# Attention scores of two streams as two 64-row tiles of TensorE, with split masks and per-slot clearing

## The reference

```python
q1, q2 = _apply_rope(q[..., :hd]), _apply_rope(q[..., hd:])      # 16 heads, hd = 8, two streams
k1, k2 = _apply_rope(k[..., :hd]), _apply_rope(k[..., hd:])
a1 = softmax(where(causal, neg, einsum('bhqd,bhkd->bhqk', q1, k1) * scale))
a2 = softmax(where(causal, neg, einsum('bhqd,bhkd->bhqk', q2, k2) * scale))
out = einsum('bhqk,bhkd->bhqd', a1 - lam * a2, v)                # then RMS norm per head, Wo, bo
```

## Time and profile before

| | us |
|---|---|
| median of 3 runs | 2002.75 (1998.85 to 2003.01) |
| the profiled execution | 2003.73 |
| its span, first to last instruction | 2001.9 |
| first feed-forward | to about 436 |
| attention | about 436 to 1566 |
| second feed-forward | about 1566 to the end |

### The profile page before, as it was taken

How to read it: one execution, slowest core, us unless ns; L and a number is a source line. 1 busy time by engine, 2 the same in 40 slices (tenths; PEclk the granted TensorE clock), 3 DMA queues, 4 the chain that set the end, 5 groups by cost and what they waited for, 6 DMA issues and landing times. The chain is left out here.

```text
span 2001.9 us, 38651 instructions
## 1 busy us (share of the span) xinstructions
PE 1846.7 (92%) x14144; PEld 1377.4 (69%) x14144; DVE 1391.4 (70%) x3443; ACT 1278.7 (64%) x1613; POOL 1035.0 (52%) x693
## 2 busy tenths in 40 slices
PE   4999999964899999999999999999998399999999
PEld 3788788843567676776776676766765277777777
DVE  5777777755767777777777777777762377777775
ACT  4777777741266666666666666666656277777776
POOL 5888888833233333424233333334221388888885
PEclk9999999986899999999999999999999599999999
DMA  3233333222222213122222222132210233333331
GB/s 106 106 106 107 106 106 106 97 83 57 56 67 57 78 49 83 52 75 62 65 68 61 73 54 79 47 82 55 69 42 14 85 125 106 107 106 106 107 101 59
DMA packets 141249, 158.76 MB, mean 79 GB/s; under 512 B 12706, under 2 KB 123442, under 8 KB 140338
## 3 DMA queue, kind: packets, MB, share of 16 engines
q1 hardware_dynamic: 141060, 156.28, 25.8%
HBM read 91.20 MB, written 14.70 MB: 53 GB/s over the span
## 5 line engine op out<-in xcount | busy, mean ns | idle before, releaser
L971 ACT ACTIVATE att_prob<-att_ring 128x1024 f32<-128x1024 f32 x384 | 389.3, 1023 | 265.6 <-PE att_ring L1186 260.9
L1096 DVE TENSOR_REDUCE att_nmax<-att_ring 128x4 f32<-128x1024 f32 (+1 forms) x384 | 457.5, 1220 | 125.9 <-PE att_ring L1186 122.7
L292 POOL TENSOR_TENSOR ffn_h_low<-ffn_h,ffn_h_high 128x1024 fp32r<-128x1024 f32 x192 | 458.5, 2401 | 95.1 <-ACT ffn_h_high L341 94.9
L479 DVE TENSOR_TENSOR ffn_h<-ffn_up,ffn_comb_wide 128x1024 f32<-128x1024 f32 x256 | 311.3, 1216 | 125.8 <-ACT ffn_up L334 121.3
L334 ACT ACTIVATE ffn_up<-ffn_up 128x1024 f32<-128x1024 f32 x256 | 258.1, 1008 | 202.9 <-PE ffn_up L567 201.6
L1186 PE MATMUL att_ring<-att_kd,att_qs 102*128 102x512 bf16 (+1 forms) x1024 | 304.4, 332 | 17.9 <-DVE att_nmax L1096 6.6
L1186 PE MATMUL att_ring<-att_qs,att_kd 102*128 102x256 bf16 (+1 forms) x2048 | 284.8, 248 | 14.6 <-DVE att_nmax L1096 8.0
L341 ACT ACTIVATE ffn_h_high<-ffn_h 128x1024 fp32r<-128x1024 f32 x256 | 269.4, 1052 | 0.7 <-DVE ffn_h L479 0.7
L1186 PE MATMUL att_ring<-att_mask,att_ident 128*128 128x256 bf16 x1024 | 262.3, 277 | 0.0
L897 POOL TENSOR_TENSOR att_qk<-att_turned 128x512 f32<-128x512 f32 x64 | 81.1, 1268 | 338.1 <-DVE att_turned L1075 338.1
L1186 PE MATMUL att_ring<-att_mask_t,att_ident 128*128 128x256 bf16 (+1 forms) x768 | 239.3, 312 | 0.0
(11 more groups left out here) (140 smaller groups left out, 2896.3 us busy)
## 6 DMA issues: line engine op xcount, KB each, us to landing
ffn_comb_wide<-ffn_comb_d SPq DMA_DIRECT2D x128, 512.0 KB, 5.6
att_qs<-att_parts SPq DMA_DIRECT2D x192, 128.0 KB
att_kd<-att_parts SPq DMA_DIRECT2D x384, 64.0 KB
ffn_x<-x SPq DMA_DIRECT2D x32, 256.0 KB, 3.2
ffn_w<-w SPq DMA_DIRECT2D x4, 1024.0 KB, 8.1
x<-ffn_out SPq DMA_DIRECT2D x16, 256.0 KB, 2.4
att_x<-x SPq DMA_DIRECT2D x32, 128.0 KB, 2.4
att_xr<-x SPq DMA_DIRECT2D x32, 128.0 KB, 2.3
```

The source lines that it names most:

```text
L292: nc.gpsimd.tensor_tensor(hts[1][:, e % NH], h[:, e % NH], hts[0][:, e % NH], ALU.subtract).then_inc(low_by_pool, 1)
L479: nc.vector.tensor_tensor(h[:, e % NH], up[:, e % NUP], comb_wide[:, b.c % NW, e].unsqueeze(1).to_broadcast([P, HE, FT]), ALU.mult).then_i ...
L971: nc.scalar.activation(prob[:, u % NP], ring[:, ORDER.index((kind, u)) % 3], ACT.Exp, scale=SCALE).then_inc(prob_ready, 1)
L1096: nc.vector.tensor_reduce(nmax[:, b, n:n + cnt], ring[:, pos % 3] .rearrange("p (a k) -> p a k", k=width), AX.X, ALU.max, negate=True).the ...
```

## The change

The stacks `qs` and `kd` become 128 rows: stream 0 in rows 0 to 63, stream 1 in rows 64 to 127; in each half 8 dimensions times 8 rows, of which six are the terms, one (`MAX_ROW`) carries a maximum or a one in three of the groups, and one (`ZERO_ROW`) stays zero. The copy with zero blocks goes: `kd` is half as large. Scores are computed per head and stream, with 64 rows each, and stream 0 and 1 write the two different banks of the buffer. The mask is added in two halves of 64 rows in each of the two tiles (`eye` times `hide`, `hide_t`), four products a unit. The order of heads and streams in `prob`, `nmax` and the output follows. A stack is filled by 12 transfers, plus one that clears the maximum rows from the zero rows from the fourth sequence on; the maxima come by 2 transfers in place of 1. The clearing is done slot by slot, the keys by DVE, the queries and v by POOL, partly behind the first normalisation; lambda is prepared behind the first key slot. Three transfers copy the masks to the upper rows.

```diff
-        qs = sb("qs", [2 * AUG, NSLOT, H, S], BF16)
-        kd = sb("kd", [2 * AUG, NSLOT, 2, H, S], BF16)
+        qs = sb("qs", [P, NSLOT, H, S], BF16)
+        kd = sb("kd", [P, NSLOT, H, S], BF16)
...
+                sp.wait_ge(setup, 2)
+                for t in (eye, hide, hide_t):
+                    sp.dma_start(t[TILE:P], t[0:TILE]).then_inc(masks_in, 16)
...
+                def set_ones(k):
+                    wait_apart(sp, keys_cleared, k + 1)
                     for s in range(2):
-                        sp.dma_start(kd[2 * ROWS + 3 * s:2 * ROWS + 3 * (s + 1), k, s].rearrange("r h q -> r (h q)"),
-                                     ones).then_inc(rows_in, 16)
+                        rows = slice(TILE * s + MAX_ROW, TILE * s + 3 * ROW_STEP, ROW_STEP)
+                        sp.dma_start(kd[rows, k].rearrange("r h q -> r (h q)"), ones).then_inc(rows_in[k], 16)
...
-                        sp.dma_start(qs[2 * ROWS:2 * AUG, k], max_rows[k].rearrange("(r h) q -> r h q", h=H)
-                                     ).then_inc(max_in, 16)
+                        for s in range(2):
+                            rows = slice(TILE * s + MAX_ROW, TILE * s + 3 * ROW_STEP, ROW_STEP)
+                            sp.dma_start(qs[rows, k], max_rows[k, 3 * H * s:3 * H * (s + 1)]
+                                         .rearrange("(r h) q -> r h q", h=H)).then_inc(max_in, 16)
...
+                        if turn.c + 1 < NSLOT:
+                            set_ones(k)
+                            wait_apart(sp, queries_cleared, k + 1)
+                            sp.wait_ge(rows_in[k], 16 * 2)
+                        if turn.c + 1 >= NSLOT:
+                            sp.dma_start(qs[MAX_ROW:P:ROW_STEP, k], qs[ZERO_ROW:P:ROW_STEP, k]).then_inc(stack_in[k], 16)
+                        for n, dst in ((0, qs), (1, kd)):
+                            wait_apart(sp, left_step, turn.at(1, 4, 3 + n))
+                            for term, pair in enumerate(TERMS):
+                                sp.dma_start(dst[term:P:ROW_STEP, k].rearrange("r (pp c) q -> r pp (c q)", c=2),
+                                             parts[:, n, pair[n]]).then_inc(stack_in[k], 16)
...
+                nc.gpsimd.memset(v[:], 0.0).then_inc(setup, 1)
+                pool.wait_ge(setup, 3)
+                nc.gpsimd.memset(v[:, :, :, :, HD:HD + 1], 1.0).then_inc(v_set, 1)
+
+                def clear_queries(k):
+                    nc.gpsimd.memset(qs[:, k].bitcast(U32), 0).then_inc(queries_cleared, 1)
+
+                clear_queries(0)
...
                 ln_rstd(Turn(-2))
+                clear_queries(1)
+                clear_queries(2)
...
-                nc.vector.memset(qs[:].bitcast(U32), 0).then_inc(dve_setup, 1)
                 nc.vector.memset(y0[:], 1.0).then_inc(dve_setup, 1)
-                nc.vector.memset(v[:], 0.0).then_inc(dve_setup, 1)
-                nc.vector.memset(kd[:].bitcast(U32), 0).then_inc(dve_setup, 1)
...
                 first = Turn(-2)
                 ln_stats(first)
                 normalise(first)
-                turns(body, -1)
+                clear_keys(0)
+                dve.wait_ge(weights_in, 16 * 12)
...
+                body(first.after())
+                clear_keys(1)
+                clear_keys(2)
+                turns(body, 0)
...
-                                for n in range(1024 // (2 * width)):
-                                    out = buf[:, n * 2 * width:(n + 1) * 2 * width].rearrange("q (s k) -> q s k", s=2)
-                                    mm(out, qs[:, k, h0 + n, b * P:(b + 1) * P], kd[:, k, :, h0 + n, 0:width], stop=False)
-                                    last = mm(out[:, :, b * P:(b + 1) * P], ident16[:], mask[:], start=False)
+                                out = buf.rearrange("q (s h k) -> q s h k", s=2, k=width)
+                                heads = 512 // width
+                                for n in range(heads):
+                                    for s in range(2):
+                                        mm(out[:, s, n], qs[tile[s], k, h0 + n, b * P:(b + 1) * P],
+                                           kd[tile[s], k, h0 + n, 0:width], start=(n == 0), stop=False)
+                                for half in range(2):
+                                    for s in range(2):
+                                        last = mm(out[:, s, :, b * P:(b + 1) * P], eye[tile[s], half],
+                                                  hide[tile[s], half, 0:heads], start=False, stop=(half == 1))
...
-                                for bank in range(2):
-                                    out = buf[:, bank * 512:(bank + 1) * 512].rearrange("k (a q) -> k a q", a=per_bank)
-                                    for i in range(per_bank):
-                                        hs = 8 * g + bank * per_bank + i + (0 if n == 2 else 4 * n)
-                                        mm(out[:, i], kd[:, k, hs % 2, hs // 2, b * P:(b + 1) * P], qs[:, k, hs // 2, q0:S],
-                                           start=(i == 0), stop=False)
-                                    last = mm(out[:, :, 0:P], ident16[:], mask_t[:, 0:per_bank], start=False)
+                                out = buf.rearrange("k (s h q) -> k s h q", s=2, h=heads)
+                                for i in range(heads):
+                                    for s in range(2):
+                                        mm(out[:, s, i], kd[tile[s], k, h0 + i, b * P:(b + 1) * P],
+                                           qs[tile[s], k, h0 + i, b * P:S], start=(i == 0), stop=False)
+                                for half in range(2):
+                                    for s in range(2):
+                                        last = mm(out[:, s, :, 0:P], eye[tile[s], half], hide_t[tile[s], half, 0:heads],
+                                                  start=False, stop=(half == 1))
```

## The result

The changed kernel takes 1902.58 us (median of 4 runs, 1901.86 to 1903.04), the kernel before 2002.67 (1998.85 to 2003.01): a ratio of 0.9504 with an interval of 0.9488 to 0.952. Forecast were 1928 us and a range of 1900 to 1968: right in sign and inside the range, but 25 us too long. The prediction's own ends were 1912 and 1953: the result lies inside only because they had been widened. The profiled execution has a span of 1900.0 us, 101.9 less than before.

A forecast was written before the change was run, and what follows sets the result against it. PE's stream was taken to set the steady turn, with DVE 8.5 us behind. Savings of 55.5 (turns), 2 (first two), 1 (drain) and 16 (start) made 74.5 us off 2003.73, 1929.2, thus a median of 1928; range 1900 to 1968.

The forecast's parts named there:

- The sum: Whole kernel: savings of 55.5 + 2 + 1 + 16 = 74.5 us.
- Units (step 1): PE's score units: 0.75 us for a large one, 0.47 for a small one, 4.3 us less per turn.
- Overlap (step 1): PE's scores: 64-row products of the two streams run side by side; a large unit 0.67 us, not 1.34.
- Passages (step 2): PE's changes between 64-row and full-size products: eight new ones per turn at 0.09 us each, 0.7 in all.
- Waits (step 3): Steady turn: PE waits on DVE's S reads in a three-buffer ring, leaving a gain of 1.85 us a turn.
- First two turns (step 3): Turns 0 and 1: only DVE's reads set the pace; 2 us gained for both.
- Drain: End of the attention: ACT's exponentials and long chains rule; 1 us gained.
- The start (step 5): Before the first S unit: moved, smaller clears and six fewer key transfers gain 16 us, ends 11 and 18.
- A: PE's scores: the pairs don't overlap, 7.2 us more per turn, 2210 us; chance 0.06.
- B: Steady turns: new waits make PE's clock fall, a loss of 1.5 us a turn, 2028 us; chance 0.05.
- C: PE's turns: weight loads and shape changes eat the gain, leaving 0.2 to 0.8 us a turn, 1970 us; chance 0.20.
- D: Steady turns: DVE doesn't hold PE, so 3.6 us a turn come off, 1876 us; chance 0.06.

The follow-up runs named there:

- the run with the early start: Kernel after with its start reordered: rstd before any clear, v and query clears behind the normalised input, lambda behind the first turn's body; 1894.22 us, ratio 0.9469.

## Why the prediction was right, and where it was off

- **The sum.** The traces differ by 101.9 us where the sum had 74.5, 27.4 less. Of these, 18.7 are the 28 even turns (2.52 us each in place of 1.85), 3.9 the first two turns, 5.5 the stretch from the last XT on and 0.8 what lies behind it; the start took 1.5 back.
- **Units (step 1): right in kind, mis-sized.** I took 0.75 and 0.47 us between the ends 0.67 and 0.89, and 0.44 and 0.56. Measured: 0.66 and 0.44, both at the cheap end. The dear end came from the spacing of 0.056 us between loads; but that is the time in which a product of 128 columns passes on the full array, not a limit of loading. In the kernel after 8 loads with their products of 128 columns take 0.23 us, 0.029 each. The term that failed in the even turns is the unit's price. With 0.66 and 0.44 in place of 0.75 and 0.47 the prediction's own walk gives 2.06 us from T7 to NT0 (measured 2.04) and about 0.4 from NT0 to XT (measured 0.46), 2.5 a turn in all. Its cheap end, given as 2.3 without passages, should have been 2.4 with them, by its own count of units on the path.
- **Overlap (step 1): right.** Full, 2.0-fold by the run with one tile. I argued it from the column tiles, and they were the right neighbour. The 3.07-fold of the Trainium skill (TensorE: Matmul & The Clock Gate, Part 3), by which a pair would have cost 1.3 slots and the kernel 1958 us, is a figure for four row tiles; a pair of 64-row tiles here costs 1.0.
- **Passages (step 2): right.** From the starts of neighbours in the two traces: the V unit takes 0.64 where it took 0.54, XT 0.37 for 0.27, the output product 0.65 for 0.55, from T2 to NT 0.09 more. About 0.1 us each, as the 0.09 taken. (Eight at twice the cost are 1.4, not the 1.6 of the prediction.)
- **Waits (step 3): right.** Walked: 0.28 us at S4, 0.67 at T10 and 0.20 at T11, from the end of one unit's columns to the next start. Read the same way, the trace has 0.39, 0.68 and 0.25, and with the cheaper units in it the walk gives 0.40, 0.70 and 0.26. (The brackets of the profile have 0.23 and 0.52, because they count from the end of the record, and none at T11.) T4 waits too, 0.42 us by its bracket; the walk has that wait, the list of signs hasn't. XT to S0 doesn't get shorter (4.87, now 4.94), nor XT to T7 (6.77 in both), T7 to NT0 falls from 15.98 to 13.94 (forecast gain 1.55, measured 2.04), NT0 to XT from 9.56 to 9.10 (0.30, 0.46). Not foreseen: the four instructions in which DVE splits the maxima into bf16 parts (128x64 each) last 0.86 us a turn (907.47 to 908.42, for example) in place of 1.30. It buys nothing that the traces show: DVE idles 2.2 us soon behind them in both kernels, ahead of the QK reads (at 881.39 and 996.66), and XT to T7 keeps its length.
- **First two turns (step 3): failed.** I gave them 2 us and they give 5.9. The step rested on one window of 4 us in which DVE was busy 3.84, and took it for both turns. Over the whole stretch before the change the share was different:

```profile
490.43:541.12 50.69, 39.97 (x232) 24.86 (x233) 36.94 (x57) 11.67 (x16) 12.88 (x12) 0.78 0.26 70
...
490.40:512.00 21.60, 16.16 (x68) 8.76 (x68) 14.91 (x21) 2.39 (x4) 5.20 (x5) 0.66 0.29 79
```

DVE was busy in 73% of it, and PE in 79% at a granted clock of 0.78, 0.66 in the first 21.6 us. After the change PE has 29.50 us of work there at 0.89, and DVE 84%. At the lower level a product of 256 columns takes 0.21 us from start to start (490.81 to 491.02 before) in place of 0.11, so that fewer columns save more there than in the even turns. How the 5.9 us divide between clock and columns no run tells apart. DVE holds this stretch as well: with halved reads it is 11 us shorter in either kernel (39.6 and 33.8 us).
- **Drain: the same fault, smaller.** From the last XT on 10.2 us come off, where the sum had 4.7 (two turns of 1.85 and 1). The window of the kernel before has PE busy 95.60 of 115.6 us at a granted clock of 0.92:

```profile
1446.10:1561.70 115.60, 95.60 (x1034) 66.16 (x1032) 50.01 (x101) 71.56 (x91) 22.59 (x29) 0.92 0.10 27
```

  After it is 80.78 of 105.5 at 0.95; 10.1 us of PE's 14.8 arrive, so that these turns and the drain were PE's more than I had taken. Whether the change brings the little more of clock or it falls out so, stays open. The same turns behind another start had 104.7 us at 0.96 (the kernel after once more) and 107.2 at 0.93 (with the old start), so up to 2.5 us of this are how it falls out; with the weighing moved, it had 0.91 and lost what the turns had gained.
- **The start (step 5): 14.5 us for 16, near in part by luck.** QK0 came at 454.48, not 451.4, and the 1.5 us held back for instruction fetching and mask transfers covered half of that; no run shows that either of the two costs anything here. I moved the clears to POOL and asked who waits for POOL, but not whom POOL's clears slow down. That costs 3.0 us in the normalisation. And of the gain, most is size, not order, which the prediction didn't separate: 6.6 us by half as many key words and 4.0 by fewer transfers, which the run with the old start shows. The forecast of what the six transfers bring (3.9) was met.
- **Rivals.** A (2210): the run with one tile has 2208, by a turn of 38.6 us in place of the 39.5 priced. B didn't come: clock 1.00 in 520.8 to 1355.2, with PE busy 92.5%. C didn't come. D asked for a turn under 29.5: not reached, but the truth, 29.80, lies nearer to it than to 30.4. Halved reads give 28.38: DVE does hold PE, by 1.4 us a turn.

## What to carry to other kernels

Products with half the rows empty could here be packed as two row tiles at no cost but about 0.1 us per change of shape, in both of the orders tried. Each tile wrote a bank of its own; nothing else was tried. Read a price of loading from a row in which loading is what limits, not from one where the product next to it is as long. When work is moved to another engine, ask three things: who waits for it, what is queued behind it, and whom it slows down where it runs beside; a clear on GpSimd held up instructions of VectorE that had nothing to do with it. And where one engine has 92% and the next holds its buffers, a saving on either arrived here by a quarter to a half (1.4 of 6.4, 1.3 of 3.5, 2.5 of 5.4 us a turn); price it by walking the ring, not by the sum of the columns.

## What the runs showed of the hardware

- Two 64-row tiles run fully side by side: 12 products in 0.66 us against 1.31 through one tile; and they do so when four score products of one tile are issued ahead of four of the other (0.65 us).
- Load and product of 128 columns of bf16 follow each other every 0.029 us over two tiles (8 in 0.23 us); with one tile it is 0.056 (8 in 0.45).
- A memset on GpSimd holds up some instructions of VectorE until its end: 0.60 us became 3.61 (128 x 128, two instructions), and an instruction on 128 x 2 numbers took 1.55. It doesn't hold every instruction up, and GpSimd's selections do it too. From the start of the run with the early start, VectorE and then GpSimd:

```profile
438.50 0.25 DVE L1057 BATCH_NORM_AGGREGATE att_mean_var<-att_stats 128x2 f32<-128x6 f32 x2
438.79 0.66 DVE L1060 TENSOR_SCALAR att_var_eps<-att_mean_var 128x2 f32<-128x2 f32 x1
...
443.11 1.76 DVE L1164 MEMSET att_kd<- 128x2048 uint32 x1 [0.37 <-issue]
...
438.54 0.29 POOL L895 TENSOR_SCALAR_AFFINE_SELECT att_eye<-att_eye 64x128 bf16<-64x128 bf16 x1
438.78 0.63 POOL L898 TENSOR_SCALAR_AFFINE_SELECT att_hide<-att_hide 64x512 bf16<-64x512 bf16 x1
...
442.79 2.66 POOL L955 MEMSET att_v<- 128x3072 f32 x1 [0.70 <-DVE att_xn L1067]
```

The aggregation beside a selection takes 0.25 us as everywhere; the addition beside the next one takes 0.66, to that one's end, where it takes 0.17 in a turn (898.04 in the kernel after). VectorE's own memset of the keys beside GpSimd's of v takes 1.76 us, as without it.
